# Six stack transfers and a row of maxima: their order in SyncE's queue of a transformer kernel

## The chip, the cores and the metric

The program runs on one core of a Trainium2 chip. The metric is the time of one execution on the device in microseconds, lower is better. A core has five engines that run in parallel, each with its own queue of instructions in order: TensorE (PE; weight loads are listed as PEld), VectorE (DVE), ScalarE (ACT), GpSimd (POOL) and SyncE (SP). SyncE computes nothing; here it waits on semaphores and issues DMAs.

## The reference

An input of 16 sequences of 256 tokens with 128 features goes through three causal attention layers with 16 heads of 8 features, and two layers of experts. Cut to what matters:

```python
# layer 1, on x (16, 256, 128)
x = x + ln(attn(ln(x)))          # phase one
# two more layers on ln(x)
for l in range(2):
    x = x + attn(ln(x) * w + b)  # phase two (l = 0), phase three (l = 1)
    h = ln(x) * w + b
    x = x + moe(h)               # l = 0: 2 of 8 experts for each token
                                 # l = 1: 2 of 8 experts for each sequence
# attn: logits = q k^T / sqrt(8), causal mask, softmax over keys, times v, times w_o
```

Everything is float32.

## The kernel before, in words

**Items.** One item is one sequence in one attention layer. There are 48, numbered v = 0 to 47: phase one has 0 to 15, phase two 16 to 31, phase three 32 to 47. Phases one and two run without a break; between two and three lie the experts of the first expert layer. The 16 heads of an item are four groups g = 0 to 3 of four heads. The items are a pipeline: a step has four slots k = 0 to 3, and in slot k every engine runs a fixed list of pieces of work that belong to different items (`pe_slot`, `act_slot`, `dve_slot`, `pool_slot`, `sp_slot`). `group(step, k, lag)` says which group of which item a slot works on, `lag` slots behind the newest. `item(step, 1)` is the next item.

**Precision and the stack.** Queries and keys are split into three bf16 parts each (`parts`): ScalarE writes the first (L525), GpSimd subtracts it (`rest`, L907), ScalarE makes the second (L563), GpSimd the third (L913, the last; semaphore `split`). Six products of parts (`TERM`, `TERMS` = 6) add up to a product close to float32. To make one bf16 matmul of them, the parts are copied into 48 of the 126 contraction rows of `stack`, one DMA for each term: `sp_stack`, L997, six DMAs of 128 KB by the profile's account. There are two stacks, by the item's parity. The six DMAs of an item raise `stack_dma`.

**Maxima.** For each group, `pe_max` (L307 mask, L309, L317) computes the logits with the queries on the partitions, from rows 0 to 125 of the stack; its first piece for group 0 waits for all six DMAs of its item (`stack_ready`). VectorE reduces them to negative maxima `negm` (L617), splits these into two bf16 parts `mparts` (L624, L626), TensorE transposes them (L361), ScalarE copies them to `mT` (L516, semaphore `mT_sb`), and SyncE copies `mT` by a DMA of 4 KB into the last two rows of the stack (L1010, semaphore `row_dma`). This is the row of maxima. One slot later `pe_scores` (L331, L336) computes the same logits transposed with the maxima already subtracted, from all 128 rows; its first piece waits for the row. Then follow exp (L505, ACT), the causal select (L898, POOL), the product with the values (L350), and later the output projection, the residual and the norms. TensorE's other steps named here: L377 is the query and key projection of the next item, L402 and L395 are transposes of the outputs of older items.

**SyncE's order.** The order is written out by hand in `sp_slot`. In each slot it sends the row of the group before (`im`, `gm`: in slot 2, group 1 of the current item). In slot 2 it also sends the next item's stack: two of the six DMAs ahead of the row, four behind it. `sp_stack` waits for `split` of its item before the first term. `alone` (L284) is a semaphore increment that changes no order, `need` (L41) a wait that is left out for values of zero or less.

Of the kernel before, what the change touches and what calls it, by code (L numbers as in the profile page):

```python
# [27 lines left out]
TERMS = len(TERM)  # L28
# [8 lines left out]
def need(eng, sem, value):  # L37

    if isinstance(value, int) and value <= 0:
        return  # L40
    eng.wait_ge(sem, value)  # L41


def build(nc, x_in, w_qk, w_v, w_o, b_qk, b_v, b_o, ln1, ln2, gate_w, gate_b, e_w1, e_b1, e_w2, e_b2, out):
# [13 lines left out]
    with ExitStack() as ctx:  # L58
# [168 lines left out]
        def item(step, d):  # L227
            n, par, phase, lo, hi = step
            if isinstance(n, int):
                v = n + d  # L230
                return Item(v, v % 2, v // B) if lo <= v < hi else None
            return Item(n + d, (par + d) % 2, phase)
# [6 lines left out]
        def group(step, k, lag):  # L239

            d, g = divmod(k - lag, NG)
            return item(step, d), g
# [38 lines left out]
        def alone(eng):  # L281


            eng.sem_inc(waited, 1)  # L284
# [697 lines left out]
        def term_rows(t):  # L982

            first = t % SPREAD + (t // SPREAD) * SPREAD * HD
            return slice(first, first + SPREAD * (HD - 1) + 1, SPREAD)

        def sp_stack(i, terms):


            if 0 in terms:  # L990
                sp.wait_ge(split, NSPLIT * i.v + NSPLIT)
                need(sp, sT_ps, 12 * (i.v - 2) + 12)
                alone(sp)
            qk = parts[:, i.par].rearrange("p w a t -> p (w a) t")
            for t in terms:
                a, b = TERM[t]
                sp.dma_start(stack[term_rows(t), i.par].rearrange("p h w t -> p (h w) t"),  # L997
                             qk[:, a:b + 4:b + 3 - a]).then_inc(stack_dma[i.par], 16)

        def sp_slot(step, k):  # L1000
            nxt = item(step, 1)
            im, gm = group(step, k, 1)
            if k == 2 and nxt:
                sp_stack(nxt, range(0, 2))
            if im:
                sp.wait_ge(mT_sb, 4 * im.v + gm + 1)
                alone(sp)
                need(sp, sT_ps, 12 * (im.v - 2) + 3 * gm + 3)
                alone(sp)
                sp.dma_start(stack[SHIFT:P, im.par, HG * gm:HG * (gm + 1), 0],  # L1010
                             mT[:, gm % 2, :]).then_inc(row_dma[gm % 2], 16)
            if k == 2 and nxt:
                sp_stack(nxt, range(2, 6))
            if k == 3 and nxt:
                sp_stack(nxt, range(6, TERMS))

        block = ctx.enter_context(nc.Block())
        RUNS = [(0, 2 * B), (2 * B, 3 * B)]
# [483 lines left out]
        @block.sync  # L1502
        def _(_):
            sp.dma_start(x_all[:, 0:8], x_dram[:, 0:8]).then_inc(x_first, 16)
            for t, d in ((ln1_s, ln1), (wqk_s, w_qk), (wv_s, w_v)):
                sp.dma_start(t[:], d).then_inc(small_ld, 16)
            sp.dma_start(x_all[:, 8:NT], x_dram[:, 8:NT]).then_inc(x_rest, 16)
            sp.wait_ge(vconst_ok, 4)
            sp.dma_start(x_routed[E * REG:E * REG + P], zeros[:]).then_inc(zeros_dma, 16)

            def filled():
                sp.wait_ge(qstack_ok, 1)
                sp.wait_ge(kstack_ok, 3)

            run_steps(sp, behind(sp_slot, -1, [filled]), *RUNS[0])
            sp_jobs()
            run_steps(sp, sp_slot, *RUNS[1])
            with sp.Fori(0, B) as b:
                sp.wait_ge(fin_x, b + 1)
                alone(sp)  # L1520
                sp.dma_start(out_dram[:, bass.ds(2 * b, 2), :], x_all[:, bass.ds(2 * b, 2), :]).then_inc(out_dma, 16)
            sp.wait_ge(out_dma, 16 * B)
# [166 lines left out]
```

## Time and profile before

| | |
|---|---|
| median of 3 runs | 1253.86 us (1253.05 to 1258.78) |
| profiled execution | 1253.16 us |
| its span, first to last instruction | 1251.4 us |
| mean granted TensorE clock | 0.954 of full speed |
| TensorE busy | 1060.6 us (85%) |
| VectorE busy | 980.6 us (78%) |
| ScalarE busy | 792.0 us (63%) |
| GpSimd busy | 685.8 us (55%) |
| DMA queue of SyncE (q1) | 99296 packets, 53.11 MB, 15.3% of 16 engines |

The span is the profiled execution's time between its first and its last instruction; 1.8 us of the execution lie around it. Phase one runs from 33 to about 310 us of the span, phase two to about 600, the first experts to about 800, phase three to about 1115, the last experts to the end. Busy shares are means over these.

### The profile page before, as it was taken

What the parts mean: (1) busy time and instruction counts of PE and PEld (TensorE: products, weight loads), DVE (VectorE), ACT (ScalarE), POOL (GpSimd) and SP (SyncE); (2) the same over time, 40 slices, a digit from 0 to 9 for tenths busy, and PEclk for the clock granted to TensorE, in tenths of its full rate; (3) what the DMA queues carried; (4) which work ended last, traced back from release to release, by engine and by line L of the source; (5) the groups of instructions that cost most, each with busy time, mean ns of one, the idle gap of its engine ahead of it and who ended that gap; (6) DMA issues with size and microseconds to landing.
All of it is one profiled execution on the core that took longest, in us unless ns stands there. A gap on an engine that the chain in (4) does not pass through costs nothing. (4 is left out here: it accounts for less than half of the span.)

```text
span 1251.4 us, 37899 instructions
## 1 busy us (share of the span) xinstructions
PE 1060.6 (85%) x10453; PEld 789.4 (63%) x10453; DVE 980.6 (78%) x2919; ACT 792.0 (63%) x1908; POOL 685.8 (55%) x1018
## 2 busy tenths in 40 slices
PE   1788999999999999999369997388889889989997
PEld 0565666666666666666269997255656556658986
DVE  3678999999998898899547765368888998876665
ACT  1566777777777767776158886256666666754554
POOL 3345555556656777776723333566676676532332
PEclk9999999999999999999679999589999899989999
DMA  5232111111111221121122222243311212100000
GB/s 144 86 110 78 50 38 42 51 52 53 53 40 45 68 66 52 55 66 43 36 72 67 69 67 74 57 116 99 85 53 53 64 39 67 53 2 10 23 18 21
DMA packets 118053, 73.07 MB, mean 58 GB/s; under 512 B 8384, under 2 KB 112960, under 8 KB 117952
## 3 DMA queue, kind: packets, MB, share of 16 engines
q1 hardware_dynamic: 99296, 53.11, 15.3%
q10 hardware_dynamic: 14560, 10.35, 3.0%
q0 software_dynamic: 4096, 8.40, 2.1%
q8 instruction: 48, 0.79, 0.3%
q14 instruction: 53, 0.43, 0.1%
HBM read 21.68 MB, written 11.60 MB: 27 GB/s over the span
## 5 line engine op out<-in xcount | busy, mean ns | idle before, releaser
L617 DVE TENSOR_REDUCE negm<-bank 128x2 f32<-128x512 f32 (+1 forms) x576 | 389.3, 679 | 82.0 <-PE bank L309 57.0
L505 ACT ACTIVATE prob<-bank 128x512 f32<-128x512 f32 x576 | 339.6, 595 | 127.1 <-PE bank L331 88.8
L898 POOL TENSOR_SCALAR_AFFINE_SELECT prob<-prob 128x512 f32<-128x512 f32 x384 | 248.6, 649 | 172.6 <-ACT prob L505 170.7
L350 PE MATMUL bank<-prob,vaug 128*32 128x256 f32 (+1 forms) x3072 | 168.6, 338 | 4.1 <-ACT oT L511 3.3
L1217 POOL COPY w_job<-w_s 128x512 f32 x104 | 69.1, 665 | 153.4 <-PE bank L1186 152.6
L317 PE MATMUL bank<-stack 126*128 126x256 bf16 x768 | 151.8, 279 | 0.0
L336 PE MATMUL bank<-stack 128*128 128x256 bf16 x768 | 150.8, 278 | 0.9 <-ACT prob L505 0.9
L1208 ACT ACTIVATE prob<-bank,b_job 128x128 f32<-128x128 f32 (+1 forms) x416 | 131.8, 400 | 17.2 <-PE bank L1186 9.9
L1197 PE MATMUL bank<-w_job,prob 128*128 128x128 f32 x1088 | 139.0, 276 | 2.5 <-issue 1.6
L1197 PEld LDWEIGHTS bank<-w_job,prob 128*128 128x128 f32 x1088 | 131.3, 192 | 6.4 <-issue 5.3
L350 PEld LDWEIGHTS bank<-prob,vaug 128*32 128x32 f32 x3072 | 81.5, 110 | 80.7 <-issue 48.9
L313 PE MATMUL bank<-maskneg,identb 128*128 128x256 bf16 x384 | 109.1, 284 | 1.7 <-issue 1.0
L307 PE MATMUL bank<-maskneg,identb 128*128 128x512 bf16 x192 | 74.5, 388 | 36.5 <-DMA stack<-parts 18.5
L516 ACT COPY mT<-bank 8x256 bf16<-8x256 bf16 x192 | 68.4, 356 | 57.7 <-PE bank L361 52.1
L331 PE MATMUL bank<-stack 128*128 128x128 bf16 x768 | 75.3, 220 | 17.3 <-DMA stack<-mT 14.7
L361 PE MATMUL bank<-identb,mparts 128*8 128x128 bf16 x384 | 53.3, 221 | 38.9 <-DVE mparts L626 37.2
L336 PEld LDWEIGHTS bank<-stack 128*128 128x128 bf16 x768 | 75.5, 99 | 13.3 <-ACT prob L505 1.5
L923 POOL DMA_INDIRECT x_routed<-hk,x_at x64 | 64.4, 1007 | 33.3 <-DVE x_at L778 14.1
L317 PEld LDWEIGHTS bank<-stack 126*128 126x128 bf16 x768 | 77.2, 101 | 8.3 <-issue 0.6
L1186 PE MATMUL bank<-oT,w_job 128*128 128x128 f32 x576 | 77.1, 277 | 0.0
L942 POOL DMA_INDIRECT y_got<-y_routed,y_at x64 | 63.8, 996 | 22.4 <-POOL y_at L939 12.3
L309 PEld LDWEIGHTS bank<-stack 126*128 126x128 bf16 x768 | 60.2, 98 | 24.8 <-issue 1.1
(181 smaller groups left out, 2122.0 us busy)
## 6 DMA issues: line engine op xcount, KB each, us to landing
stack<-parts SPq DMA_DIRECT2D x288, 128.0 KB
w_s<-e_w ACTq DMA_DIRECT2D x32, 256.0 KB, 3.0
oT<-x_routed SPq DMA_DIRECT2D x72, 64.0 KB, 1.7
y_routed<-oT SPq DMA_DIRECT2D x36, 128.0 KB, 1.9
stack<-mT SPq DMA_DIRECT2D x192, 4.0 KB
out<-x_all SPq DMA_DIRECT2D x16, 128.0 KB, 1.8
b_all<-e_b ACTq DMA_DIRECT2D x2, 512.0 KB, 8.4
x_routed<-hk,x_at POOLq DMA_INDIRECT x64
```

The source lines that it names most:

```text
L307: nc.tensor.matmul(o, identb[:], maskneg[:], start=True, stop=False, skip_group_check=True)
L313: nc.tensor.matmul(o[:, :, P:T], identb[:], maskneg[:, 0:2], start=True, stop=False, skip_group_check=True)
L317: m = nc.tensor.matmul(o[:, h], q[:, hh, P:T], k[:, hh, :], start=False, stop=True, skip_group_check=True)
L331: m = nc.tensor.matmul(bk[:, h * P:(h + 1) * P], k[:, p0 + h, P:T], q[:, p0 + h, P:T], start=True, stop=True)
L336: m = nc.tensor.matmul(bk[:, h * T:(h + 1) * T], k[:, hh, 0:P], q[:, hh, :], start=True, stop=True)
L350: m = nc.tensor.matmul(o, w, (prob0, prob1)[kb][:, g % 2, h], start=kb == 0, stop=kb == 1, skip_group_check=True)
L505: nc.scalar.activation(o, s, ACT.Exp, scale=SCALE).then_inc(exp_done, 1)
L617: nc.vector.tensor_reduce(o, s, AX.X, ALU.max, negate=True).then_inc(max_done, 1)
L898: nc.gpsimd.affine_select(out=t, in_=t, compare_op=ALU.is_ge, fill=0.0, base=0, pattern=[[0, HG], [1, P]], channel_multiplier=-1).then_inc ...
L1186: m = nc.tensor.matmul(bank[2 * par + c // 2][:, (c % 2) * T:(c % 2) * T + width], w1_job[:, par, c * P:(c + 1) * P], rows, start=True, st ...
L1197: m = nc.tensor.matmul(y_bank[par][:, t * P:(t + 1) * P], hid[:, par, c, t * P:(t + 1) * P], w2_job[:, par, c], start=(c == 0), stop=(c == ...
L1208: nc.scalar.activation(hid[:, par, c, 0:width], bank[2 * par + c // 2][:, (c % 2) * T:(c % 2) * T + width], ACT.Gelu, bias=b1_job[:, par, ...
```

## The change

In slot 2, where the next item belongs to phase two or three, the row of maxima is sent first and all six stack DMAs behind it. Items of phase one keep the order two, row, four. The branch for k = 3 was empty (six terms) and is dropped.

```diff
         def sp_slot(step, k):
             nxt = item(step, 1)
             im, gm = group(step, k, 1)
+            ahead_of_row = 2 if nxt and nxt.phase == 0 else 0
             if k == 2 and nxt:
-                sp_stack(nxt, range(0, 2))
+                sp_stack(nxt, range(0, ahead_of_row))
             if im:
                 sp.wait_ge(mT_sb, 4 * im.v + gm + 1)
                 alone(sp)
...
                 sp.dma_start(stack[SHIFT:P, im.par, HG * gm:HG * (gm + 1), 0],
                              mT[:, gm % 2, :]).then_inc(row_dma[gm % 2], 16)
             if k == 2 and nxt:
-                sp_stack(nxt, range(2, 6))
-            if k == 3 and nxt:
-                sp_stack(nxt, range(6, TERMS))
+                sp_stack(nxt, range(ahead_of_row, TERMS))
```

With an empty range `sp_stack` issues nothing and waits for nothing.

## Rows read from the trace of the kernel before

**Rows 1.** Windows: stretch, length, busy us (instructions) of PE PEld DVE ACT POOL, PEclk, DMA.

```profile
294.00:575.70 281.70, 261.00 (x2869) 181.54 (x2869) 256.07 (x819) 202.69 (x462) 194.56 (x281) 1.00 0.20 56
823.50:1094.40 270.90, 233.10 (x2426) 155.71 (x2427) 235.56 (x580) 178.08 (x403) 177.93 (x253) 0.96 0.24 67
```

**Rows 2.** Line L307 in two windows: its matmuls, first and last start; idle time before.

```profile
L307 PE MATMUL bank<-maskneg,identb x65: 376/379/390, 294.0 to 575.7; 128*128 128x512 bf16 x65
...
  DMA stack<-parts: 1.8, 4
...
L307 PE MATMUL bank<-maskneg,identb x57: 379/379/390, 824.1 to 1094.4; 128*128 128x512 bf16 x57
...
  DMA stack<-parts: 6.0, 6
```

**Rows 3.** Timeline of SyncE: start us, us, what, count [idle before <-releaser].

```profile
513.98 1.36 SPq L997 DMA_DIRECT2D stack<-parts  x2
515.82 0.52 SPq L1010 DMA_DIRECT2D stack<-mT  x1
516.38 2.62 SPq L997 DMA_DIRECT2D stack<-parts  x4
520.02 9.78 SPq L1010 DMA_DIRECT2D stack<-mT  x3
```

**Rows 4.** Timeline of GpSimd and ScalarE at the same place.

```profile
512.62 1.16 POOL L913 TENSOR_TENSOR parts<-rest,parts 128x512 bf16<-128x512 f32 x1
514.76 0.36 ACT L516 COPY mT<-bank 8x256 bf16<-8x256 bf16 x1 [0.46 <-PE bank L361]
519.42 0.36 ACT L516 COPY mT<-bank 8x256 bf16<-8x256 bf16 x1 [0.21 <-issue]
```

**Rows 5.** Timeline of TensorE and VectorE at the same place and later.

```profile
518.18 0.40 PE L331 MATMUL bank<-stack 128*128 128x128 bf16 x4 [0.38 <-DMA stack<-mT]
522.17 0.38 PE L307 MATMUL bank<-maskneg,identb 128*128 128x512 bf16 x1
524.99 0.44 PE L402 MATMUL bank<-ident,on 128*128 128x128 f32 x2 [0.21 <-DVE on L636]
527.99 0.69 DVE L617 TENSOR_REDUCE negm<-bank 128x4 f32<-128x512 f32 x1 [0.48 <-PE bank L309]
532.41 0.28 PE L361 MATMUL bank<-identb,mparts 128*8 128x128 bf16 x2 [0.82 <-DVE mparts L626]
```

**Rows 6.** Timelines of SyncE and TensorE where TensorE waits for a stack.

```profile
166.74 1.35 SPq L997 DMA_DIRECT2D stack<-parts  x2
...
174.76 0.39 PE L307 MATMUL bank<-maskneg,identb 128*128 128x512 bf16 x1 [0.17 <-DMA stack<-parts]
...
25.87 4.18 SPq L997 DMA_DIRECT2D stack<-parts  x6
...
33.24 0.61 PE L307 MATMUL bank<-maskneg,identb 128*128 128x512 bf16 x1 [5.17 <-DMA stack<-parts]
...
797.98 4.27 SPq L997 DMA_DIRECT2D stack<-parts  x6
...
805.86 0.61 PE L307 MATMUL bank<-maskneg,identb 128*128 128x512 bf16 x1 [4.41 <-DMA stack<-parts]
```

**Rows 7.** Waits of TensorE, 310 to 575 and 823 to 1095: us, times, longest.

```profile
PE bank L331 <- DMA stack<-mT: 4.9, 11, 0.6
...
PE bank L331 <- DMA stack<-mT: 3.5, 3, 2.8
```

**Rows 8.** Timelines of SyncE and TensorE, an item of phase three.

```profile
972.18 1.35 SPq L997 DMA_DIRECT2D stack<-parts  x2
...
981.72 0.38 PE L307 MATMUL bank<-maskneg,identb 128*128 128x512 bf16 x1
```

**Rows 9.** Windows of two items of phase three, columns as in rows 1.

```profile
923.00:941.80 18.80, 15.98 (x174) 10.84 (x175) 16.60 (x43) 12.20 (x28) 12.89 (x19) 1.00 0.21 57
961.70:981.70 20.00, 17.40 (x176) 11.36 (x174) 17.97 (x44) 12.87 (x30) 13.36 (x20) 0.91 0.19 53
```

## The prediction

> **What bounds the kernel now.** I read the views in the order of the questions. First the busy time of the engines in the two stretches that the change touches [rows 1]: phase two from the first group of its item 16 on, and phase three. VectorE is busy for 256.07 of 281.70 us and 235.56 of 270.90, TensorE for 261.00 and 233.10. Nobody is idle, so what matters is the ring of dependences that gives an item its period: (575.7 - 294.0) / 16 items = 17.6 us in phase two and (1094.4 - 824.1) / 14 = 19.3 us in phase three, by the first and last start of L307 [rows 2]. The same rows say how seldom the stack now stops TensorE at L307, 1.8 us in phase two and 6.0 in phase three (weight loads and matmuls added, so about half of that as time).
>
> Then one item of phase two, on SyncE's queue [rows 3]: two stack DMAs at 513.98, the row of group 1 at 515.82, four more stack DMAs at 516.38 (issued by 519.00), the row of group 2 at 520.02. What released them [rows 4]: POOL's last part was ready at 513.78 (512.62 + 1.16), the mT copy of group 1 at 515.12 (514.76 + 0.36). So the two DMAs ahead of the row sit in a time in which the row doesn't exist yet; they use 1.3 us of waiting. The row's own delay through them is 0.70 us (515.12 to 515.82), against 0.24 where nothing stands before it (mT ends at 519.78, row at 520.02) [rows 3, 4].
>
> Then the two readers on TensorE [rows 5]. The scores of group 1 start at 518.18 after 0.38 us of idle time that the row ended. The next item's first maxima start at 522.17 with no idle time shown, but the stack was only just there. In phase one, at this order of issue, TensorE waits for the stack and starts 8.02 us after the first issue (166.74 to 174.76) [rows 6]; 522.17 is 8.19 us after 513.98. The slack of the stack is therefore about 0.2 us. **The stack has almost no slack, and the row has some 0.4 us of loss.** That is what the change trades.
>
> **What it gives.** Row of group 1: issue at 515.12 + 0.24 = 515.36 for 515.82, and no stack packets ahead of it. The idle time before the scores goes: 4.9 us over phase two, 3.5 us over phase three, of which 2.8 us is one wait [rows 7]. At most 8.4 us, if nothing else held the period.
>
> **What it moves.** All six stack DMAs now stand behind the wait for mT of group 1. Nothing is added or removed: six DMAs and one row per item before and after, the empty step at k = 3 is no instruction. Queued behind SyncE's new wait are the six DMAs and then the row of group 2; who waits for them is L307 of the next item and the scores of group 2.
> - First stack issue: 515.12 (mT) + 0.24 (to the row's issue) + 0.52 (the issue of the row at 515.82) + 0.20 (what SyncE needs from a satisfied wait to the issue, 513.78 to 513.98) = 516.08. With 0.48 for the last step (515.34, end of the second stack DMA, to 515.82, with mT there already) it is 516.36. I take 516.2, which is 2.2 us later than now [rows 3, 4].
> - From the first issue to TensorE's start: no item of phases two and three issues six in a row today, but the first item of phase one and that of phase three do. 25.87 to 33.24 is 7.37 us, 797.98 to 805.86 is 7.88 us, with TensorE waiting both times [rows 6]. The second runs beside GpSimd's row transfers, as the changed items do. I take 7.5. It is less than today's 8.02, as the row and the gap no longer lie in the middle.
> - So TensorE can start at 516.2 + 7.5 = 523.7 instead of 522.17: 1.5 us later.
> - What the delay gives back: TensorE's short wait for VectorE at L402, 0.21 us, is taken up. Nothing else is: from there TensorE works without a break until it waits 0.82 us at 532.41 for `mparts`, and in this stretch VectorE itself waits for TensorE (0.48 at 527.99) [rows 5]. So mT of group 1, which now starts the stack, comes later by the same amount: the delay lies in the ring of the period and comes back in every item, 1.3 us each.
> - Row of group 2: SyncE is done with the stack at 516.2 + 4.18 (six issues [rows 6]) = 520.4 instead of 519.0; the row goes at 520.6 instead of 520.02 and lands behind the stack as now, while its scores stand behind the later L307. It costs nothing of its own. Groups 3 and 0 are issued into an empty queue as before.
>
> **Sum, phase two.** Items 16 to 31: 16 x 1.3 = 20.8. In the items 16 to 21 the kernel doesn't have the wait of L402 to give back and I give the stack no slack (some of the idle times of [rows 2] lie there), 0.3 us more each: +1.8. Together +22.6.
>
> **Sum, phase three.** Item 32 has no row beside its stack, so 15 items are touched. They fall into two kinds. Where the stack is just in time, the cost is as above or a little more, 1.6 us; where TensorE is late for other reasons there is slack: in the item at 972.18, TensorE starts 9.54 us after the first issue (981.72), and by the same steps the stack would be there at 972.18 + 2.2 + 7.5 = 981.9, 0.2 us late [rows 8]. I take half of the items for each kind: 7 x 1.6 + 7 x 0.3 = 13.3. The one item with the wait of 2.8 us gains, since its row stands ahead of the stack transfers that it now waits behind; I take 2.0 of the 2.8. Net +11.3.
>
> Profiled execution 1253.16 (span 1251.4; the median of the runs is 1253.86) + 22.6 + 11.3 = 1287; I say **1286**.
>
> **A rule that speaks for more.** The Trainium skill, "DMA: Bandwidth & Descriptors", section "Rules for kernel authors", advises to issue a DMA early and wait for it late, so that its fixed cost overlaps with compute. The trace agrees: the first two stack DMAs now overlap with the 1.3 us in which SyncE would wait for mT, and the change gives that up. The same page, section "Anatomy of one DMA", gives about 2.0 us fixed and bytes at 436 GB/s (measured for GpSimd's DMAs). By it the six transfers of 128 KB would be done some 2 us behind their last issue, and issue would be the limit. The trace doesn't agree: 7.37 us from the first issue is 3.2 us behind the end of the six issues, and six times 128 KB in these 7.37 us is 107 GB/s.
>
> **The rivals.**
> - *Issue-bound stack.* If the transfers kept up with their issue, the last of six, issued 5 x 4.18 / 6 = 3.5 us after the first, would land like the row, whose scores start 518.18 - 515.82 = 2.36 us after its issue [rows 3, 5], or up to 0.6 us later for its size: TensorE would start 5.9 to 6.5 us after the first issue, at 522.1 to 522.7. That is 0 to 0.5 us per item, and with 0.2 us some 31 x 0.2 = +6, less part of the one gain of 2: 1257 to 1262. Against it: both measured sets of six [rows 6]. 0.09.
> - *Faster.* The place is the scores of group 1. If the six DMAs landed within 522.17 - 516.2 = 5.97 us of their first issue, L307 would lose nothing and the row's 8.4 us would be won: 1245. From 5.97 us up it loses. Measured is 7.37 and 7.88 [rows 6]; also, VectorE is busy through the wait, so the gain would be passed on only in part. 0.04.
> - *No change*: gain and loss cancel, or the slack at L307 is larger than I read: 1254. 0.05.
> - *Clock.* TensorE would stand for 1.5 to 2 us before L307 (the row's 0.4 us are moved there too) and 0.8 us at L361. In some items of phase three the granted clock drops already: an item of 20.0 us has a mean of 0.91, which is (1 - 0.91) x 20.0 / 0.5 = 3.6 us at the lower level (1.2 GHz of 2.4), where one at 1.00 throughout takes 18.8 [rows 9]. If the new wait brought such a stretch to every second one of 31 items, it would cost 15 x 1.2 = 18 us more: 1304. In phase two the clock is 1.00 throughout [rows 1]. 0.12.
> - The forecast: 0.70, by itself 1275 to 1298 (7.0 to 7.9 us for the six, all or half of the late items of phase three spared).
>
> **Range and chances.** The low end takes in part of the issue-bound case: 1265. The high end takes in half of the clock's case: 1302. A change of under 0.5% (6.3 us) can't be told from none here. Faster 0.04; same 0.07 (no change and a part of the issue-bound case); slower 0.89.
>
> **What would show it.** In the changed kernel's SyncE queue, the row ahead of six stack issues that take about 4.2 us without a gap, the first some 1.1 us after the mT copy. No idle time at L331 for the row in group 1. Idle time at L307 ended by the stack DMA in nearly every item from 16 on, 1.5 to 2 us each, where there is almost none now. An item of phase two of about 19 us for 17.6. The forecast is wrong if L307 shows little wait, which would mean that the six land within 6 us; if the period doesn't grow by what L307 waits, VectorE has more to catch up than I read; and if it grows by more, the granted clock should be below 1.00 in phase two.

## The result and the profile after

The changed kernel takes 1311.09 us (median of 4 runs, 1310.78 to 1312.18) for 1255.51 (4 runs): a ratio of 1.0443 with a 95% interval of 1.0414 to 1.0471. The forecast was 1286 us, 1265 to 1302. It had the direction and the trade, but not the clock; the measured time lies 9 us above the range.

The page of the profile after, its head, the busy time and the slices (TensorE, VectorE and granted clock):

```profile
span 1309.3 us, 37899 instructions
...
PE 1073.6 (82%) x10453; PEld 795.6 (61%) x10453; DVE 975.1 (74%) x2919; ACT 792.8 (61%) x1908; POOL 687.0 (52%) x1018
...
PE   1798999998888888888559997377778898879997
...
DVE  3688999999778778777556774357878888875675
...
PEclk9999999999999999999779999689999898999999
```

VectorE's digits of phase two have gone from 9 and 8 to 7 and 8: every engine has about as much to do as before and waits longer. Line L307 in phase two and in phase three (from the first L307 of item 33), as in [rows 2], and then the same waits of phase two (310 to 610) as time of TensorE's matmuls alone:

```profile
L307 PE MATMUL bank<-maskneg,identb x65: 376/379/609, 291.7 to 609.1; 128*128 128x512 bf16 x65
...
  DMA stack<-parts: 46.3, 24
...
L307 PE MATMUL bank<-maskneg,identb x57: 379/387/606, 861.7 to 1151.5; 128*128 128x512 bf16 x57
...
  DMA stack<-parts: 39.2, 19
...
PE bank L307 <- DMA stack<-parts: 31.2, 16, 3.2
```

An item of phase two takes (609.1 - 291.7) / 16 = 19.8 us for 17.6, one of phase three (1151.5 - 861.7) / 14 = 20.7 for 19.3. The idle time that the stack ends was 1.8 and 6.0 us and is 46.3 and 39.2 (weight loads and matmuls added); as time it is 31.2 us in phase two, in each of the 16 items. One item of phase two in the timelines, to be read against [rows 3] to [rows 5]; GpSimd's last part, then SyncE, then TensorE:

```profile
537.33 1.16 POOL L913 TENSOR_TENSOR parts<-rest,parts 128x512 bf16<-128x512 f32 x1
...
535.63 5.03 SPq L1011 DMA_DIRECT2D stack<-mT  x2
540.98 4.01 SPq L997 DMA_DIRECT2D stack<-parts  x6
545.47 0.50 SPq L1011 DMA_DIRECT2D stack<-mT  x1
...
541.90 0.38 PE L307 MATMUL bank<-maskneg,identb 128*128 128x512 bf16 x1
542.11 0.39 PE L309 MATMUL bank<-stack 126*128 126x128 bf16 x4
542.34 0.39 PE L331 MATMUL bank<-stack 128*128 128x128 bf16 x4
...
548.38 0.39 PE L307 MATMUL bank<-maskneg,identb 128*128 128x512 bf16 x1 [1.70 <-DMA stack<-parts]
```

The parts are ready at 538.49; the first of the six goes at 540.98, 2.49 us later, where it went 0.20 us later. The scores of group 1 (L331) follow L309 without a wait: the row's 0.38 us are gone. L307 of the next item starts 7.40 us after the first issue and has stood for 1.70 us.

**The ring in three legs.** For each of the 31 touched items (16 to 31, 33 to 47) I took from the timelines the start of L307 of the item before, the end of the mT copy of group 1, the first stack issue, and the start of L307. Where the record of an L307 is missing, its place is that of the first L309 less 0.22 us. Sums over the 31 items in us, each from one profiled execution:

| kernel | L307 to mT | mT to first issue | first issue to L307 | all |
|---|---|---|---|---|
| before | 339.1 | -37.1 | 268.3 | 570.2 |
| changed | 352.2 | 32.6 | 244.1 | 628.9 |
| e1, TensorE kept busy | 339.5 | 32.7 | 248.5 | 620.6 |
| e2, order two, row, four; late | 338.9 | 11.9 | 257.3 | 608.1 |
| e3, one ahead of the row | 337.2 | -33.0 | 278.8 | 583.0 |
| four stack DMAs for six, before / changed | 335.6 / 335.5 | -33.6 / 32.3 | 269.0 / 193.4 | 571.0 / 561.3 |
| three stack DMAs for six, before / changed | 335.5 / 338.1 | -33.4 / 32.8 | 265.1 / 189.0 | 567.2 / 559.9 |

The change costs 58.6 us by it: +69.7 on the leg that it lengthens, -24.2 on the last one, and **+13.1 on the first leg, which it doesn't touch**. (The spans differ by 57.9; the rest of the program is within 1 us of itself in sum.)

The first leg is the granted clock. Windows of five items of the changed kernel, columns as in [rows 1], each from one L307 to the next:

```profile
404.90:424.70 19.80, 16.59 (x183) 11.61 (x183) 15.86 (x55) 12.75 (x29) 14.41 (x20) 1.00 0.19 55
424.70:447.10 22.40, 18.17 (x182) 12.43 (x182) 16.23 (x55) 12.92 (x29) 14.25 (x20) 0.92 0.18 50
447.10:466.90 19.80, 16.61 (x182) 11.52 (x182) 16.09 (x55) 12.93 (x29) 12.91 (x19) 1.00 0.20 55
506.30:527.50 21.20, 18.00 (x182) 12.26 (x182) 15.91 (x55) 12.92 (x29) 13.86 (x20) 0.91 0.18 50
527.50:548.40 20.90, 18.14 (x183) 12.46 (x184) 15.82 (x55) 12.91 (x29) 13.60 (x19) 0.92 0.18 51
```

Of these five, the items with a mean below 1.00 take 20.9 to 22.4 us, the others 19.8. TensorE's timeline at the start of the second:

```profile
424.69 0.49 PE L307 MATMUL bank<-maskneg,identb 128*128 128x512 bf16 x1 [1.94 <-DMA stack<-parts]
424.97 0.63 PE L309 MATMUL bank<-stack 126*128 126x128 bf16 x4
425.40 0.63 PE L331 MATMUL bank<-stack 128*128 128x128 bf16 x4
425.83 2.02 PE L377 MATMUL bank<-xT,wqk_s 128*128 128x256 f32 x4
```

Four L309 take 0.63 us for 0.39, L377 2.02 for 1.08 at the full level: TensorE comes back from its wait at the lower of its two levels (1.2 GHz of 2.4), in the very stretch where the ring goes through it. The granted clock fell within 0.8 us of the item's first L307 in 8 of the 31 turns (the L307 of items 17, 22, 26, 27, 29, 33, 34 and 38). Their first legs are 1.1 to 2.6 us longer than in the kernel before, 12.5 us together, which is nearly all of the 13.1.

### The profile page after: what moved, and what is told of

Its sections match the earlier page's. It is cut to its first block, busy times and chain, and to the rows that moved or that the text cites. A ratio compares the mean times of both kernels' runs of the same rounds, so it can differ in the third digit from the quotient of the medians.

```text
span 1309.3 us, 37899 instructions
## 1 busy us (share of the span) xinstructions
PE 1073.6 (82%) x10453; PEld 795.6 (61%) x10453; DVE 975.1 (74%) x2919; ACT 792.8 (61%) x1908; POOL 687.0 (52%) x1018
## 4 chain that ended last, share of the span: by engine, by line
PE 27%; DVE 6%; DMA 6%; issue 4%; SPq 4%; ACT 2%; POOL 1%; DVEq 0%; POOLq 0%; ACTq 0%
PE bank L1196 9%; PE bank L1185 9%; DMA stack<-parts 5%; SPq L997 3%; DVE negm L617 1%; PE bank L377 1%; PE bank L350 1%; PE bank L317 1%; PE bank L336 1%; PE bank L408 1%; PE bank L307 1%; DVE f_all L675 1%; PE bank L361 1%; PE bank L1257 1%; PE bank L313 1%
## 5 line engine op out<-in xcount | busy, mean ns | idle before, releaser
L505 ACT ACTIVATE prob<-bank 128x512 f32<-128x512 f32 x576 | 339.5, 595 | 173.7 <-PE bank L331 135.1
L1216 POOL COPY w_job<-w_s 128x512 f32 x104 | 69.7, 671 | 153.4 <-PE bank L1185 152.6
L307 PE MATMUL bank<-maskneg,identb 128*128 128x512 bf16 x192 | 75.8, 395 | 89.0 <-DMA stack<-parts 70.0
L307 PEld LDWEIGHTS bank<-maskneg,identb 128*128 128x128 bf16 x192 | 19.0, 99 | 110.3 <-DMA stack<-parts 45.1
L331 PE MATMUL bank<-stack 128*128 128x128 bf16 x768 | 77.2, 224 | 8.6 <-DMA stack<-mT 6.9
L317 PEld LDWEIGHTS bank<-stack 126*128 126x128 bf16 x768 | 77.2, 100 | 8.4 <-issue 0.6
L309 PE MATMUL bank<-stack 126*128 126x128 bf16 x768 | 77.2, 224 | 0.0
```

Source lines behind the costliest of these rows:

```text
L307: nc.tensor.matmul(o, identb[:], maskneg[:], start=True, stop=False, skip_group_check=True)
L309: m = nc.tensor.matmul(o[:, h], q[:, p0 + h, 0:P], k[:, p0 + h, 0:P], start=False, stop=True, skip_group_check=True)
L317: m = nc.tensor.matmul(o[:, h], q[:, hh, P:T], k[:, hh, :], start=False, stop=True, skip_group_check=True)
L505: nc.scalar.activation(o, s, ACT.Exp, scale=SCALE).then_inc(exp_done, 1)
```

## The experiments

Each kernel ran in rounds against the kernel before; the ratio is to that.

### Is the extra cost the clock?

> The changed kernel, with seven more mask products on TensorE (0.21 us each, 1.5 us together) ahead of its wait for the stack at L307 in phases two and three; they write the bank that the real mask product then overwrites. Theory (ring and clock): the wait at L307 is as long as before, the products lie inside it, and the stretches at 0.5 of the clock that began within 1 us of L307 (items 17, 22, 26, 27, 33, 34, 38 of the changed kernel, where the leg from L307 to mT took 12 to 14 us for 10.2 to 11.7) go: about 9 x 1.4 = 13 us less, 1298 us. Rival (the longer legs are something else, DMA or GpSimd): 1311 us as the changed kernel, clock in phase two at 1.00 without a gain. Rival (the ring has no slack at L307): above 1311.

```diff
-            if g == 0 and u == 0:
-                pe.wait_ge(stack_dma[i.par], stack_ready(i))
             need(pe, max_done, unit(i, g, u) - 2)
             bk = max_bank[(g + u) % 2]
+            if g == 0 and u == 0:
+                if i.phase > 0:
+                    for _ in range(7):
+                        nc.tensor.matmul(bk[:].rearrange("p (h k) -> p h k", h=HG), identb[:], maskneg[:],
+                                         start=True, stop=False, skip_group_check=True)
+                pe.wait_ge(stack_dma[i.par], stack_ready(i))
```

1302.35 us, ratio 1.0347 (1.0299 to 1.0395), against 1.0443 (1.0414 to 1.0471) for the change alone: faster with more work, by about 1% (12 us) by the ratios and by 8.7 us by the medians. The windows from 300 to 600 us, the changed kernel and then e1:

```profile
300.00:600.00 300.00, 254.47 (x2703) 175.44 (x2704) 238.94 (x773) 191.41 (x434) 185.83 (x268) 0.97 0.18 50
```

```profile
300.00:600.00 300.00, 273.01 (x2816) 184.59 (x2859) 243.97 (x789) 194.34 (x441) 190.32 (x273) 0.99 0.18 51
```

TensorE is busy for 273 of 300 us for 254, the clock is at 0.99 for 0.97, and the first leg is back at 339.5 us, the 339.1 of the kernel before. The rivals (another cause of the long legs; no slack at L307) fall. The first leg gives back 12.7 us, as expected, but the last one is 4.4 us longer (248.5 for 244.1), so by the legs the gain is 8.2 us and not 13. Why the last leg grew was not taken apart; in phase two TensorE still waits for the stack behind the products in 9 items of 16, so in the others the products may be what it is late with.

### The late start or the order?

> The kernel before with its order two, row, four, but SyncE waits for mT of group 1 ahead of the first two stack DMAs too, in phases two and three. Theory (the stack's late start is the price, not the order): the first issue stands 0.2 us behind mT instead of 1.1 us ahead of it, the way from it to L307 stays 8.0 to 8.3 us, so an item takes 10.8 + 0.2 + 8.2 = 19.2 us in phase two for 17.9, and the whole 1253 + 31 x 1.2 = 1290 us, up to 1305 with clock drops. TensorE waits at L331 for the row and hardly at L307. Rival (six DMAs in a row behind the row are what costs): 1254 to 1260 us.

```diff
+            if k == 2 and nxt and nxt.phase > 0 and im:
+                sp.wait_ge(mT_sb, 4 * im.v + gm + 1)
             if k == 2 and nxt:
                 sp_stack(nxt, range(0, 2))
```

1292.78 us, ratio 1.0272 (1.0230 to 1.0314). The old order with the new wait costs 2.7%, most of the 4.4% of the change. Waits of TensorE from 300 to 600 us:

```profile
PE bank L331 <- DMA stack<-mT: 24.9, 16, 1.7
...
PE bank L309 <- DMA stack<-parts: 3.7, 7, 1.3
```

The row is now the late one, since its issue stands behind two late stack issues: 24.9 us at L331, and little at the head of the item (L309 where the record of L307 is missing). The leg from mT to the first issue grew by 49.0 us, the last leg shrank by 11.0. The rival, that the six in a row cost, would have given 1254 to 1260. What the change costs beyond e2 goes with its still later first issue (32.6 us for 11.9 on the middle leg) and with its longer first leg.

> The changed kernel with one stack DMA ahead of the row and five behind it, in phases two and three. Theory (what counts is how many transfers have to go after the row): the five start about 2.0 us after the first issue and need 0.75 us less than six (7.5 us), so L307 can start 8.7 us after the first issue instead of 8.2: 0.5 us an item and few clock drops, 1265 to 1275 us. Rival (any wait at L307 brings the clock down and costs like the whole change): 1295 us or more.

```diff
-            ahead_of_row = 2 if nxt and nxt.phase == 0 else 0
+            ahead_of_row = 2 if nxt and nxt.phase == 0 else 1
```

1268.00 us, ratio 1.0084 (1.0057 to 1.0111). With one DMA ahead of the row most of the loss is gone; the last leg is 9.0 us for 8.65 (8.73 in phase two, where 8.7 was expected). TensorE's wait for the stack from 300 to 580 us (L309 where the record of L307 is missing):

```profile
PE bank L309 <- DMA stack<-parts: 12.9, 15, 1.9
```

That is 0.9 us per item, and the first leg keeps to 337.2 us: these waits, one of 1.9 us among them, brought the clock down nowhere in phase two. The rival falls.

### Does the row in front gain anything?

Here two or three of the six products are left out in all phases, so that the logits are less exact; the times are of less work.

> Control: the kernel before with four stack DMAs per item for six (terms four and five are left out, so the logits are less exact), order two, row, two, in all phases. Theory (ring): the stack is there about 6.5 us after its first issue for 8.0, ahead of TensorE, so no waits at L307; the items of phase one were bound by it by 0.1 to 0.2 us only. 1245 to 1252 us. Rival (transfers bind nothing): 1254.

> The changed kernel with the same four DMAs: row, four in phases two and three. Theory (threshold at about 6 us from the first issue): four transfers need 7.4 - 2 x 0.75 = 5.9 us, so L307 can start 2.2 + 5.9 = 8.1 us after the time of the old first issue, where TensorE comes by itself (8.2, or 7.8 with the row's wait gone): within 0.5% of the four-DMA control, for the +4.4% that it costs with six. Rival (the order costs by itself, through the wait for mT in SyncE's queue): 2% or more above the control.

```diff
-STACK_DMAS = TERMS
+STACK_DMAS = 4
...
-                sp_stack(nxt, range(2, 6))
-            if k == 3 and nxt:
-                sp_stack(nxt, range(6, TERMS))
+                sp_stack(nxt, range(2, 4))
```

(and `range(ahead_of_row, 4)` in the changed kernel.) 1241.91 us for the old order (ratio 0.9868, 0.9835 to 0.9901) and 1236.59 for the new one (0.9847, 0.9816 to 0.9878). The order that costs 4.4% with six DMAs costs nothing with four. The last leg of the new order is 193.4 / 31 = 6.2 us. The control is 3 us faster than I had expected. The 9.7 us between the two rows of the table are not the change's gain: the control's profiled execution was its slowest (1246.79 us), with three items of 21.0 to 21.4 us at the head of phase three, and in phase two alone the new order is 0.7 us longer by the legs.

> Control with three stack DMAs (terms three, four and five are left out), order two, row, one. Theory: as with four, 1243 to 1250 us; what is left binds by the row of group 1 and by VectorE.

> The changed kernel with three DMAs: row, three. Theory: the stack is now early in both orders (2.2 + 5.2 = 7.4 us), so what is left of the change is its gain, the row of group 1 without stack packets ahead of it: at most 0.4 us in ten items and 2 to 3 us in one, 0 to 6 us below the three-DMA control. Rival (the row was no loss, VectorE hides it): same as the control.

The same edit with 3 in place of 4. 1238.21 us (0.9853, 0.9825 to 0.9880), 5 us below the range that I had given the control, and 1229.18 (0.9767, 0.9736 to 0.9797): the new order is now 9 us faster, and the intervals don't meet. Waits of TensorE from 300 to 560 us, old order and new:

```profile
PE bank L361 <- DVE mparts L626: 12.5, 15, 0.9
PE bank L331 <- DMA stack<-mT: 4.3, 10, 0.7
```

```profile
PE bank L361 <- DVE mparts L626: 12.5, 15, 0.9
...
PE bank L309 <- DMA stack<-parts: 0.8, 1, 0.8
```

The wait at L331 is gone and nothing as long has taken its place. The row's wait is a true loss that comes back once nothing else binds: by the legs 3.0 us in phase two and 4.3 in phase three. I had expected 0 to 6 us of it, because VectorE is busy meanwhile; by the medians it is more.

### Forecasting another kernel from the legs

> The row ahead of all six in phase one as well. Theory (the ring: L307 to mT 10.2 us, mT to first issue 1.0, first issue to L307 7.45, by the changed kernel's items 16 to 21): an item of phase one takes 18.7 us for 17.3, 14 or 15 items x 1.4 = 20 us more, with clock drops up to 30: 1331 to 1341 us. Rival (phase one has less work around the row and can absorb it): 1311 to 1316.

```diff
-            ahead_of_row = 2 if nxt and nxt.phase == 0 else 0
+            ahead_of_row = 0
```

1342.96 us, ratio 1.0702 (1.0656 to 1.0748), 2 us above the range. In its trace an item of phase one (items 2 to 15) takes 19.3 us for 17.4. Waits of TensorE from 54 to 320 us:

```profile
PE bank L307 <- DMA stack<-parts: 30.9, 14, 5.1
```

The ring absorbs nothing there either. The miss is in the same place as that of the forecast: four stretches at the lower clock reach into these items, and the first leg is 10.6 us for the 10.2 that I had taken.

### Two attempts to be faster than the kernel before

> The kernel before, but ScalarE itself issues the rows of maxima behind its copy of mT (in slot 0 one exp later), and SyncE issues all six stack DMAs in a row as soon as they are split, in all phases. Theory: both sides of the trade at once. L307 can start 7.4 to 7.5 us after the first issue for 8.0 (phase one waits for it: 16 x 0.5 = 8 us less) and the row of group 1 goes out 0.5 us sooner; ScalarE pays about 0.3 us of waiting for its own copy and 0.35 us of issue for each of 192 rows beside 63% busy time. 1240 to 1250 us. Rival (ScalarE's queue is in the ring: exp, qkf and the split stand behind the issue): 0.65 us for three of the four groups in 48 items, up to 1253 + 90 us. Rival (the row's packets now share the engines with the six and land as late as now): 1245 to 1254.

```diff
+        def act_row(i, g):
+            act.wait_ge(mT_sb, 4 * i.v + g + 1)
...
+            act.dma_start(stack[SHIFT:P, i.par, HG * g:HG * (g + 1), 0],
+                          mT[:, g % 2, :]).then_inc(row_dma[g % 2], 16)
...
             if k == 2 and nxt:
-                sp_stack(nxt, range(0, 2))
-            if im:
...
+                sp_stack(nxt, range(TERMS))
```

1299.33 us, ratio 1.0340 (1.0289 to 1.0391): much slower. Waits of TensorE from 300 to 600 us:

```profile
PE bank L331 <- DMA stack<-mT: 12.2, 11, 1.6
PE bank L309 <- DVE negm L630: 5.2, 10, 0.6
PE bank L369 <- ACT hT L606: 4.8, 12, 0.6
```

Both of the rivals are in it: the rows land late beside six stack transfers (12.2 us at L331, for 4.9 in [rows 7]), and TensorE now waits for ScalarE. Each row's issue by ScalarE is listed with 0.63 to 0.66 us where I had taken 0.35. How the loss divides between the two was not taken apart.

> The kernel before, with six more mask products (0.21 us each) on TensorE in slot two of phase three, where it waits 1.5 us at L307 for VectorE and then 0.86 us at L361; they go to the bank of the next scores, which overwrite them. Theory (the clock falls after these waits; items with a drop take 19.7 to 20.2 us, items without one 18.8): the seven drops in items 36 to 44 go and with them 7 x 1.1 = 8 us, 1246 us. Rival (TensorE is not bound there, the drop is harmless and the long items are long for another reason): 1254. Rival (the products come in the way of the real ones): up to 1260.

```diff
+            if k == 2 and cur and ie and cur.phase == 2:
+                need(pe, exp_done, unit(ie, ge, 0) - 2)
+                for _ in range(6):
+                    nc.tensor.matmul(exp_bank[ge % 2][:].rearrange("p (h k) -> p h k", h=HG), identb[:], maskneg[:],
+                                     start=True, stop=False, skip_group_check=True)
             if cur:
                 pe_max(cur, k, 0)
```

1253.60 us, ratio 0.9967 (0.9943 to 0.9991). Windows of phase three, the kernel before and then this one:

```profile
845.00:1060.00 215.00, 184.57 (x1913) 123.06 (x1912) 190.55 (x471) 141.12 (x320) 147.66 (x209) 0.95 0.24 66
```

```profile
845.00:1060.00 215.00, 196.04 (x2001) 128.68 (x1999) 187.29 (x476) 142.90 (x322) 149.28 (x211) 0.98 0.24 66
```

The clock rises from 0.95 to 0.98, and the time gives back 0.3%, not the 8 us expected. The windows split this in two. Items 33 to 35, and then items 36 to 44, of the kernel before:

```profile
824.10:883.40 59.30, 48.91 (x514) 32.40 (x514) 48.44 (x117) 37.24 (x85) 38.80 (x55) 0.97 0.39 107
883.40:1060.20 176.80, 152.68 (x1567) 101.60 (x1568) 156.50 (x386) 115.43 (x261) 120.73 (x171) 0.94 0.20 56
```

and of this one:

```profile
823.50:888.00 64.50, 56.27 (x532) 36.57 (x533) 47.18 (x117) 37.23 (x84) 38.36 (x54) 0.89 0.34 96
888.00:1058.20 170.20, 156.74 (x1622) 102.41 (x1621) 153.36 (x387) 115.88 (x262) 121.32 (x172) 1.00 0.22 59
```

In items 36 to 44 the theory holds: the clock's drops (six there; the seventh that I had counted lies in item 33) are all gone, the clock is at 1.00 for 0.94, and 6.6 us come back, 1.1 us for each drop. So the price of a drop that I had read from two items of phase three [rows 9] is confirmed, also where TensorE waits for VectorE. But items 33 to 35 take 5.2 us more: the clock is at 0.89 there for 0.97, and TensorE waits 7.1 us at L331 for the row where it waited 3.2. The four-DMA control has three such items of 21.0 to 21.4 us in the same place without any added product, so the products alone are not shown to make them; what does stays open. On the whole it is barely faster than the kernel before and no case for a change.

## Why the prediction was right or wrong

**The bottleneck and the trade: right.** The stack had almost no slack and the row a small loss. e2 and e3 show the first by making the stack late in other ways, the three-DMA pair shows the second.

**The first issue 2.2 us later: right.** It is 69.7 / 31 = 2.25 us.

**From the first issue to L307, 7.5 us: too low.** It is 7.45 us in items 16 to 21 and 7.93 in items 22 to 31, where single items take 7.4 to 8.9 us; 7.87 over all 31, 11.6 us in sum. The two sets of six that I had to go by [rows 6] were 7.37 and 7.88, and the second, beside GpSimd's transfers, was the one like the touched items. That these transfers are the cause is argued only; no run takes them away.

**"What the delay gives back: 0.21 us": this step failed.** The first leg was to be 0.2 us shorter in items 22 to 31, 2.1 us together, and to stay as it was in the others. It is 13.1 us longer over the 31 items (0.42 us each). I had written the reason down as the rival *Clock*, priced it at 18 us and given it 0.12, with "in phase two the clock is 1.00 throughout" as the reason against it. But that row tells of a kernel in which TensorE hardly waits; the change is what makes it wait. In phase two the window of 300 us has a mean clock of 0.97 for 1.00, and e1 shows that the loss is the clock's. The likeliest case should have held part of it. In number the rival was near: 8 items, not 15, but 1.1 to 2.6 us each, 12.5 us for its 18. This step and the one before it are together as large as what the forecast lacks, 58.6 us by the legs for 33.9.

**By phases.** Phase two was forecast at +22.6 and is +35.7: by legs +6.7, +36.0 and -7.0, where the forecast's own steps give about -2, +35 and -11. Phase three was forecast at +11.3 and is +22.9: by legs +6.4, +33.7 and -17.2. The +6.4 is again the first leg, with three of the eight drops. The last leg is 8.0 us there, not 7.5, which is 7.6 us over 15 items; the slack that I had spared half of the items for was less than I read. In the changed kernel L307 waits for the stack in 12 of the items from 33 on, 23.7 us:

```profile
PE bank L307 <- DMA stack<-parts: 23.7, 12, 4.4
PE bank L307 <- DVE negm L617: 16.2, 12, 1.6
```

The item whose wait of 2.8 us at L331 was to give back 2.0 us is 0.5 us longer than before. The wait is gone and its last leg is 1.8 us shorter (8.7 for 10.5), but its first leg is 1.6 us longer at the lower clock, its first issue comes 0.8 us later against mT, and TensorE stands for 2.99 us before the next L307.

**A reading that was off.** The 294.0 of [rows 2] is the first L307 of item 15, not of item 16 as I wrote. The 16 periods from there to 575.7 are those in which the stacks of items 16 to 31 are sent, so the sum does not change.

**The rivals.** *Issue-bound stack* and *faster* set their point of decision at about 6 us from the first issue to L307. The four-DMA pair lies on it (6.2 us, no loss) and the three-DMA pair has 6.1 us with L307 hardly waiting, and a gain of 9 us where 8.4 was the bound. The mechanism of *faster* was right, and its condition is false with six transfers.

## What to carry to other kernels

Before you put a small urgent transfer ahead of large ones, look at what the large ones do in the meantime: here they filled a wait of 1.3 us, and the move set their start back by that wait and the small one's issue, 2.2 us in each turn of the ring, to save 0.4. Split the period of a pipelined loop into legs between events that must follow each other; then each edit has one leg, and a leg that moves without an edit points to what you left out. Where a change makes TensorE wait, count the granted clock of the changed kernel, not that of the old one; a drop cost 1.1 to 2.6 us here. And when a cure gives back less than its price says, split the stretch before you doubt the price: another part of it may have grown.

## What the runs showed of the hardware

The granted clock fell after some waits and not after others of the same size: TensorE stood for 1.94 us before 424.69 and came back at the lower level, and for 3.16 us before 447.11 and came back at the full one:

```profile
447.11 0.39 PE L307 MATMUL bank<-maskneg,identb 128*128 128x512 bf16 x1 [3.16 <-DMA stack<-parts]
```

With waits of about 0.9 us per item (e3) it stayed at the full level in phase two. What decides was not isolated.

Mask products that nobody reads, put into TensorE's waits, made a kernel faster by 1% (e1). In another (e8) they took the drops out of nine items and 6.6 us with them, but three other items grew by 5.2 us, and 0.3% was left.
